# Local attention: the additive mask moved behind the score products, and cut to the key columns that it can change

## The chip, the cores and the metric

One core of a Trainium2 chip runs the whole program. The metric is the device time of one launch, in microseconds (us), lower is better. The kernel is a chain of eight stages, a small transformer with a residual stream of 2048 tokens x 256 features that stays in the on-chip memory. The change touches one of them, the fifth in order of execution, causal local attention.

## The reference

The stage takes the normalised residual `x` as query and `ctx_1024` as key and value (8 batches, 256 tokens, 16 heads of width 16, window 64). A block of 64 queries sees its own block of 64 keys and the one before it; key j is hidden from query i if j comes later than i, and for the first block of a batch the whole previous block is hidden.

```python
qb = q.reshape(b, h, nb, w, d) * scale            # w = 64, nb = 4
kw = look_around(kb)                              # [.., 128, d]: the block before, then the own block
vw = look_around(vb)
mask = (t[:, :, None] >= kt[:, None, :]) & (kt[:, None, :] >= 0)
sim = jnp.einsum('bhnwd,bhnjd->bhnwj', qb, kw)
sim = jnp.where(mask[None, None], sim, -jnp.finfo(sim.dtype).max)
attn = jax.nn.softmax(sim, axis=-1)
out = jnp.einsum('bhnwj,bhnjd->bhnwd', attn, vw)
...
return x @ W_out.T + b_out
```

So of the 128 key columns of a block, the first 64 are hidden altogether or not at all, and only the last 64 have the diagonal mask.

## The kernel before

The stage is `stage_local_attention` (L1930 to L2290). A step n covers two neighbouring query blocks of one batch: batch b = n // 2, u = n % 2, 16 steps in all. In a step the heads lie in four row groups r of 32 partitions (`RT = 4`), so the score products use 32 rows of the array; each row group has a PSUM bank of its own, `scores[r]`, of 128 x 512: partitions are two heads x 64 queries, columns are four (block, half of the features) pairs j x 128 keys. The four banks are handled in two halves, r = 0, 1 (half 0) and r = 2, 3 (half 1), so there are 32 score halves in all.

All steps are written out, without a loop on the chip. `walk` fixes the order on every engine. In one turn of it for step n:

```python
score(n, 1); turn(n, 0)
score(n + 1, 0)
if u == 0: prep_x(b + 1)
weigh(n - 1)
if u == 0: prep_k(b + 1)
turn(n, 1)
if u == 1 and b >= 1: final(b - 1)
if u == 0 and b >= 2: finish(b - 2)
```

- `score` (L2057): TensorE. It waits for the spread queries (`q_ready`), and for each bank until ScalarE has read it. Per bank it first writes the mask with one matmul of a bf16 identity against `masks[:, u > 0]` (L2066, 128 rows, 512 columns, start=True), and then adds eight fp32 score records onto it (L2072: four matmuls, each two passes in the trace; 32 rows, 128 columns; the two banks of a half take turns).
- VectorE takes the negated maximum of each of the four column groups of a bank (L2184), ScalarE the exponentials (L2142, four of 128x128 to a bank).
- `turn` (L2082): eight fp32 128x128 transposes in a half, into one of two `turned` banks each; ScalarE copies them out (L2151, to `eT`).
- `weigh` (L2099): 128 small fp32 records, 128 rows x 32 columns of the array, values and row sums, into the bank `av`; then VectorE takes reciprocals (L2191) and the quotient (L2193).
- `prep_x`, `prep_k` (L2053): four 128x128 transposes of the next batch's queries or keys into the one `misc` bank; `final` (L2112) the output product of the batch before; `finish` on VectorE normalises two tiles (L217) and takes their largest values (L2212).

On VectorE the order is that of `walk` too; on ScalarE it is exponents(n, 1), the copies of turn(n, 0), the queries of prep_x, exponents(n + 1, 0), the keys of prep_k, the copies of turn(n, 1).

Of the kernel before, what the change touches and what calls it, by code (L numbers as in the profile page):

```python
# [12 lines left out]
P = 128  # L13
# [14 lines left out]
KD = D // P  # L28
# [1901 lines left out]
def stage_local_attention(nc, core, ins):  # L1930
# [4 lines left out]
    HEADS, W = 16, 64  # L1935
# [9 lines left out]
    with ExitStack() as ctx:  # L1945
# [4 lines left out]
        ident16 = st.sb("ident16", [P, P], BF16)  # L1950
        masks = st.sb("masks", [P, 2, 4, P], BF16)
# [4 lines left out]
        qd = st.sb("qd", [P, 2, KD, NU, 2 * W])  # L1956
        kT = st.sb("kT", [P, 2, KD, W + S])
# [17 lines left out]
        def walk(prep_x, prep_k, score, turn, weigh, final, finish):  # L1975
            prep_x(0)
            prep_k(0)
            score(0, 0)
            for n in range(STEPS + 1):
                b, u = divmod(n, NU)  # L1980
                if n < STEPS:
                    score(n, 1)
                    turn(n, 0)
                if n + 1 < STEPS:
                    score(n + 1, 0)
                if u == 0 and b + 1 < B:
                    prep_x(b + 1)
                if n >= 1:
                    weigh(n - 1)
                if u == 0 and b + 1 < B:  # L1990
                    prep_k(b + 1)
                if n < STEPS:
                    turn(n, 1)
                if u == 1 and b >= 1:
                    final(b - 1)
                if u == 0 and b >= 2:
                    finish(b - 2)
            final(B - 1)
            finish(B - 1)
# [4 lines left out]
        @block.sync  # L2004
        def _(sp):
            wm = Walk(misc, sp)
            ctx_d = ins["ctx_1024"]

            def load(b):
                sp.dma_start(xs[:, b % 2, 0:2, :], core.xn[:, 2 * b:2 * b + 2, :]).then_inc(xs_in[b % 2], 16)  # L2010
                sp.dma_start(xs[:, b % 2, 2:4, :], ctx_d.rearrange("b (h p) d -> p b h d", p=P)[:, b, :, :]
                             ).then_inc(xs_in[b % 2], 16)
                if b >= 2:
                    sp.wait_ge(vz_ready, b - 1)
                sp.dma_start(vn[W:P, b % 2, 0, :], ctx_d[b, 0:W, :]).then_inc(vn_in[b % 2], 16)
                for nb in range(1, UNITS):
                    sp.dma_start(vn[:, b % 2, nb, :], ctx_d[b, W * (nb - 1):W * (nb + 1), :]).then_inc(vn_in[b % 2], 16)

            sp.wait_ge(const, 3)
            load(0)  # L2020
            sp.dma_start(wo[:, :, :], ins["L2_xattn_W_out"].rearrange("(r p) k -> p r k", p=P)).then_inc(small_in, 16)
            sp.dma_start(bias[:, :], ins["L2_xattn_b_out"].partition_broadcast(P)).then_inc(small_in, 16)
            load(1)
            wm.skip(1)

            def prep_k(b):
                wm.when_filled(wm.use())
                if b + 2 < B:
                    load(b + 2)

            walk(lambda b: wm.skip(1), prep_k, nothing, nothing, nothing, lambda b: wm.skip(1), nothing)

        @block.tensor
        def _(pe):
            ws, wt, wa, wm = (Walk(banks, pe) for banks in (scores, turned, av, misc))
            pe.wait_ge(const2, 2)
            kept, score_bank, turned_bank = {}, {}, {}

            def weights():
                pe.wait_ge(small_in, 32)  # L2040
                ps, filled, _ = wm.fill()
                for kt in range(KD):
                    for r in range(2):
                        last = nc.tensor.transpose(ps[:, (kt * 2 + r) * P:(kt * 2 + r + 1) * P],
                                                   wo[:, r, kt * P:(kt + 1) * P], core.ident[:, :])
                last.then_inc(filled, 1)

            def prep(b, part):
                pe.wait_ge(xs_in[b % 2], 32 * (b // 2 + 1))
                ps, filled, kept[b] = wm.fill()  # L2050
                for kt in range(KD):
                    for h in range(2):
                        last = nc.tensor.transpose(ps[:, kt * S + h * P:kt * S + (h + 1) * P],  # L2053
                                                   xs[:, b % 2, 2 * part + h, kt * P:(kt + 1) * P],
                                                   core.ident[:, :])
                last.then_inc(filled, 1)

            def score(n, half):
                b, u = divmod(n, NU)
                pe.wait_ge(q_ready, n + 1)  # L2060
                if u == 0 and half == 0:
                    wm.when_read(kept[b])
                banks = [(r, ws.fill()) for r in SETS[half]]
                for r, (ps, _, use) in banks:
                    score_bank[n, r] = use
                    nc.tensor.matmul(ps[:, :], ident16[:, :], masks[:, int(u > 0), :, :], start=True, stop=False)  # L2066
                for j in range(4):
                    nb, kt = divmod(j, KD)
                    lo = W * (NU * u + nb)
                    for r, (ps, filled, _) in banks:  # L2070
                        rows = slice(R * r, R * (r + 1))
                        last = nc.tensor.matmul(ps[:, j * P:(j + 1) * P], qd[rows, n % 2, kt, nb, :],  # L2072
                                                kT[rows, b % 2, kt, lo:lo + P], start=False, stop=(j == 3))
                        if j == 3:
                            last.then_inc(filled, 1)

            def turn(n, half):
                for r in SETS[half]:
                    ws.when_read(score_bank[n, r])
                    ps, filled, turned_bank[n, r] = wt.fill()  # L2080
                    for j in range(4):
                        last = nc.tensor.transpose(ps[:, j * P:(j + 1) * P], e[:, n % 2, r, j, :], core.ident[:, :])  # L2082
                    last.then_inc(filled, 1)

            def weigh(n):
                b, u = divmod(n, NU)
                pe.wait_ge(vz_ready, b + 1)
                for r in range(RT):
                    wt.when_read(turned_bank[n, r])
                ps, filled, _ = wa.fill()  # L2090
                for j in range(4):
                    nb, kt = divmod(j, KD)
                    for what in range(2):
                        o = (4 * what + j) * W
                        for h in range(2):
                            for r in range(RT):
                                lhs = (ones[:, h, :, :] if what else
                                       vz[:, b % 2, NU * u + nb, RT * kt + r, 2 * h:2 * h + 2, :])
                                last = nc.tensor.matmul(ps[R * r:R * (r + 1), o:o + W],  # L2099
                                                        lhs.rearrange("p a d -> p (a d)"),  # L2100
                                                        eT[:, n % 2, r, j, h * W:(h + 1) * W],
                                                        start=(h == 0), stop=(h == 1))
                last.then_inc(filled, 1)

            def final(b):

                if b == B - 1:
                    wa.when_all_read()
                ps, filled, _ = wm.fill()
                for h in range(2):  # L2110
                    for kt in range(KD):
                        last = nc.tensor.matmul(ps[:, h * D:(h + 1) * D], aoT[:, b % 2, kt, h * P:(h + 1) * P],  # L2112
                                                woT[:, kt, :], start=(kt == 0), stop=(kt == KD - 1))
                last.then_inc(filled, 1)

            weights()
            walk(lambda b: prep(b, 0), lambda b: prep(b, 1), score, turn, weigh, final, nothing)

        @block.scalar
# [1339 lines left out]
```

## Time and profile before

| | |
|---|---|
| median of 3 runs | 2153.23 us (2150.3 to 2153.67) |
| the profiled execution's own time | 2154.32 us |
| its span in the profile | 2152.6 us |
| mean granted TensorE clock | 0.937 of full speed |
| TensorE matmul busy, of the span | 87% |
| VectorE busy | 59% |
| ScalarE busy | 39% |
| GpSimd busy | 13% |

The span is that of the instructions in the trace, and the device time lies a little above it. In the profile PE is TensorE's matmuls, PEld its weight loads, DVE is VectorE, ACT is ScalarE, POOL is GpSimd. A matmul's duration in the trace reaches to the modelled arrival of its last result, so matmuls that follow each other overlap in the rows: with x records in a merged row, the last one starts at the row's start plus the row's length less one record's duration. The attention stage runs from about 1331 to 1477 us of the span.

### The profile page before, as it was taken

To read this page: it belongs to the slowest core of one execution; us is meant where nothing else is said; L and a number is where in the kernel's file an instruction comes from. 1 tells how busy PE (TensorE), PEld (TensorE's weight loads), DVE (VectorE), ACT (ScalarE), POOL (GpSimd) and SP (SyncE) were. 2 spreads that over 40 slices of the span, in tenths; PEclk is the share of its full clock that TensorE was granted. 3 is DMA by queue.
4 is the path that set the end of the run, shared out by engine and by line. 5 is a ranking of instruction groups with operands and counts; after the bars stand their busy time and mean duration, and the time that the engine had idled before them with its cause. 6 is when DMAs were issued, how large, how long until landed. Compare 5 with 4: busy or idle time off the path is not lost. (4 is left out here: it accounts for less than half of the span.)

```text
span 2152.6 us, 39260 instructions
## 1 busy us (share of the span) xinstructions
PE 1881.7 (87%) x13712; PEld 1521.6 (71%) x13713; DVE 1274.2 (59%) x4672; ACT 839.8 (39%) x2287; POOL 276.1 (13%) x501
## 2 busy tenths in 40 slices
PE   8699997999998989999999995996940977999978
PEld 6466665677667979999999884884520866777745
DVE  7767764877883541111111152775778527999988
ACT  3333334655653111111111112872477513444469
POOL 2001112000000160000000253330000230000022
PEclk9899998999998999999999996998975987999989
DMA  5111112121113431230320112201000031111100
GB/s 177 64 44 55 55 54 72 40 79 40 40 40 122 171 113 44 79 140 26 140 83 24 46 48 68 71 22 60 0 1 0 0 119 43 34 35 37 34 8 33
DMA packets 104818, 127.05 MB, mean 59 GB/s; under 512 B 32080, under 2 KB 83800, under 8 KB 102872
## 3 DMA queue, kind: packets, MB, share of 16 engines
q1 hardware_dynamic: 93512, 109.35, 15.3%
q0 software_dynamic: 3072, 8.39, 1.2%
q10 hardware_dynamic: 8080, 7.35, 1.0%
q8 instruction: 85, 1.39, 0.3%
q14 instruction: 69, 0.57, 0.1%
HBM read 86.39 MB, written 34.54 MB: 56 GB/s over the span
## 5 line engine op out<-in xcount | busy, mean ns | idle before, releaser
L1721 DVE TENSOR_TENSOR me_h<-me_sg,me_ps_u 128x512 f32<-128x512 f32 x106 | 72.6, 687 | 288.1 <-PE me_ps_u L1544 272.8
L1677 ACT ACTIVATE me_sg<-me_ps_g 128x512 f32<-128x512 f32 x106 | 63.3, 597 | 370.9 <-PE me_ps_g L1544 340.8
L1260 ACT ACTIVATE ca_e<-ca_scored,ca_neg_max 128x256 f32<-128x256 f32 x256 | 127.2, 499 | 108.3 <-DVE ca_neg_max L1319 108.3
L1544 PE MATMUL me_ps_g<-me_x_turned,me_w 128*128 128x128 f32 x1184 | 145.1, 276 | 1.9 <-issue 1.9
L1544 PE MATMUL me_ps_u<-me_x_turned,me_w 128*128 128x128 f32 x1184 | 145.4, 276 | 0.0
L1544 PEld LDWEIGHTS me_ps_g<-me_x_turned,me_w 128*128 128x128 f32 x1184 | 141.1, 192 | 4.6 <-issue 2.9
L1551 PE MATMUL me_ps_y<-me_w,me_h 128*128 128x256 f32 x592 | 140.0, 379 | 0.0
L1544 PEld LDWEIGHTS me_ps_u<-me_x_turned,me_w 128*128 128x128 f32 x1184 | 139.4, 193 | 0.0
L2922 ACT ACTIVATE sc_y_all<-ss_v 128x16 f32<-128x16 f32 x256 | 60.9, 238 | 159.9 <-DVE ss_v L2985 159.9
L1551 PEld LDWEIGHTS me_ps_y<-me_w,me_h 128*128 128x128 f32 x592 | 106.8, 190 | 11.4
L1319 DVE CUSTOM_DVE_ANT_0 ca_scored<-ca_main,ca_mask_add 128x256 f32<-128x256 f32 x256 | 92.9, 419 | 22.4 <-PE ca_main L1200 22.4
L3070 PE MATMUL ss_idle<-ident 128*128 128x128 f32 x648 | 90.5, 286 | 0.0
L2954 DVE SCALAR_TENSOR_TENSOR ss_left<-ss_nq,ss_v 128x16 f32<-128x16 f32 x446 | 90.3, 202 | 0.0
L2390 PE MATMUL ig_ps<-nw_int_wT,ig_xT 128*128 128x384 f32 x256 | 87.3, 496 | 0.0
L1922 POOL DMA_INDIRECT me_rows<-moe_y_list,me_slot x32 | 31.2, 974 | 432.9 <-DVE carrier L81 424.6
L3070 PEld LDWEIGHTS ss_idle<-ident 128*128 128x128 f32 x648 | 79.8, 196 | 6.5 <-issue 3.4
L2142 ACT ACTIVATE la_e<-la_scores,la_mx 128x128 f32<-128x128 f32 x256 | 70.5, 422 | 30.1 <-DVE la_mx L2184 30.1
L1212 PE MATMUL ca_turned<-ident,ca_e 128*128 128x128 f32 x512 | 70.2, 281 | 13.4 <-DVE ca_e L1332 13.4
L1745 DVE COPY me_y<-me_ps_y 128x256 f32<-128x256 f32 x37 | 15.7, 425 | 108.0 <-PE me_ps_y L1551 108.0
L1212 PEld LDWEIGHTS ca_turned<-ident,ca_e 128*128 128x128 f32 x512 | 57.8, 143 | 29.9 <-DVE ca_e L1332 22.2
L1332 DVE TENSOR_SCALAR ca_e<-ca_e,ca_rsums 128x256 f32<-128x256 f32 x256 | 74.9, 356 | 2.2
L1544 PE MATMUL me_ps_g<-me_xT,me_w13s 128*128 128x128 f32 x512 | 67.2, 284 | 5.6 <-issue 4.8
(441 smaller groups left out, 4392.9 us busy)
## 6 DMA issues: line engine op xcount, KB each, us to landing
me_w<-in_L_ffn_w_e SPq DMA_DIRECT2D x24, 1024.0 KB, 7.4
ss_gb<-scan_g_band SPq DMA_DIRECT2D x15, 512.0 KB, 3.7
ca_k_list<-kv_out SPq DMA_DIRECT2D x28, 256.0 KB, 2.4
ca_v_list<-kv_out SPq DMA_DIRECT2D x28, 256.0 KB, 2.4
moe_x_list<-me_zeros SPq DMA_DIRECT2D x1, 5248.0 KB, 21.8
me_x_tile<-moe_x_list SPq DMA_DIRECT2D x38, 128.0 KB, 2.0
moe_y_list<-me_y ACTq DMA_DIRECT2D x37, 128.0 KB, 1.7
ca_kT<-ca_k_list SPq DMA_DIRECT2D x4, 1024.0 KB, 5.2
```

Source lines behind the costliest of these rows:

```text
L1212: last = nc.tensor.transpose(ps[:, jt * S + it * P:jt * S + (it + 1) * P], e[:, g % 3, e_, it, jt * P:(jt + 1) * P], core.ident[:, :])
L1260: nc.scalar.activation(e[:, g % 3, e_, it, :], scored[:, g % 2, e_, it, :], ACT.Exp, scale=-1.0, bias=neg_max[:, g % 2, n:n + 1], accum_ou ...
L1319: last = nc.vector.tensor_tensor_reduce(scored[:, g % 2, e_, it, :], ps[:, it * S:(it + 1) * S], mask_add[:, b, :], -1.0, -NEG, ALU.add, A ...
L1332: last = nc.vector.tensor_scalar(e[:, g % 3, e_, it, :], e[:, g % 3, e_, it, :], rsums[:, par, n:n + 1], None, ALU.mult)
L1544: last = nc.tensor.matmul(ps[:, j * P:(j + 1) * P], w[:, n, kt, f:f + P], x[:, kt, :], start=(kt == 0), stop=(kt == KD - 1))
L1551: last = nc.tensor.matmul(ps_y[:, 0:D], h[:, c, j, :], w[:, f, :], start=(f == 0), stop=(f == FT - 1))
L1677: nc.scalar.activation(sg[:, c, :], ps_g[c][:, :], ACT.Silu).then_inc(done, 1)
L1721: nc.vector.tensor_tensor(h[:, c, :, :].rearrange("p j n -> p (j n)"), sg[:, c, :], ps_u[c][:, :], ALU.mult).then_inc(done[c], 1)
L2142: last = nc.scalar.activation(e[:, n % 2, r, j, :], scores.ps[r][:, j * P:(j + 1) * P], ACT.Exp, bias=mx[:, n % 2, r, j:j + 1])
L2390: last = nc.tensor.matmul(ps[2 * w + c][:, 0:HALF], xT[:, par, kt, :], wT[:, w, kt, c * HALF:(c + 1) * HALF], start=(kt == 0), stop=(kt == ...
L2954: return nc.vector.scalar_tensor_tensor(out, nq[:, t % 2, :].unsqueeze(2).broadcast_to([P, C, n]), 1.0, src, ALU.add, ALU.mult)
L3070: nc.tensor.matmul(idle[:, 0:P], core.ident[:, :], core.ident[:, :], start=True, stop=True)
```

## The change

The mask matmul of each bank moves from ahead of the score matmuls to behind them, and writes only columns that can be masked. In the last 64 keys of each of the four column groups the diagonal mask is added, a matmul with 4 x 64 = 256 columns, in every bank. In steps with u = 0 a second matmul of 2 x 64 = 128 columns hides the block before the first one. The first score matmul now starts the accumulation, and the last mask matmul ends it and signals `filled`.

```diff
                 for r, (ps, _, use) in banks:
                     score_bank[n, r] = use
-                    nc.tensor.matmul(ps[:, :], ident16[:, :], masks[:, int(u > 0), :, :], start=True, stop=False)
                 for j in range(4):
                     nb, kt = divmod(j, KD)
                     lo = W * (NU * u + nb)
                     for r, (ps, filled, _) in banks:
                         rows = slice(R * r, R * (r + 1))
-                        last = nc.tensor.matmul(ps[:, j * P:(j + 1) * P], qd[rows, n % 2, kt, nb, :],
-                                                kT[rows, b % 2, kt, lo:lo + P], start=False, stop=(j == 3))
-                        if j == 3:
-                            last.then_inc(filled, 1)
+
+                        nc.tensor.matmul(ps[:, j * P:(j + 1) * P], qd[rows, n % 2, kt, nb, :],
+                                         kT[rows, b % 2, kt, lo:lo + P], start=(j == 0), stop=False)
+
+                for r, (ps, filled, _) in banks:
+                    columns = ps[:, :].rearrange("p (j s) -> p j s", j=4)
+                    last = nc.tensor.matmul(columns[:, :, W:2 * W], ident16[:, :], masks[:, 1, :, W:2 * W],
+                                            start=False, stop=(u > 0))
+                    if u == 0:
+                        last = nc.tensor.matmul(columns[:, 0:KD, 0:W], ident16[:, :], masks[:, 0, 0:KD, 0:W],
+                                                start=False, stop=True)
+                    last.then_inc(filled, 1)
```

## Rows read from the trace of the kernel before

**Rows 1.** The head of the profile's page

```profile
span 2152.6 us, 39260 instructions
```

**Rows 2.** Busy time by stretches of the stage: us, then busy us of each engine

```profile
1331.00:1345.00 14.00, 12.93 (x88) 9.19 (x90) 3.87 (x6) 8.59 (x30) 5.50 (x9) 0.67 0.28 86
1345.00:1360.00 15.00, 14.99 (x370) 12.31 (x368) 9.42 (x12) 13.66 (x45) 5.01 (x8) 1.00 0.20 66
1360.00:1375.00 15.00, 15.00 (x366) 12.57 (x363) 9.58 (x19) 11.19 (x37) 4.08 (x10) 1.00 0.20 59
1382.00:1399.00 17.00, 16.85 (x380) 13.91 (x376) 13.12 (x23) 13.31 (x44) 6.23 (x11) 1.00 0.19 61
```

**Rows 3.** Groups of instructions of the stage: score and mask matmuls

```profile
L2072 PE MATMUL la_scores<-la_kT,la_qd 32*128 32x128 f32 x512 | 39.1, 293 | 0.0
L2066 PE MATMUL la_scores<-la_masks,la_ident 128*128 128x512 bf16 x64 | 20.4, 402 | 0.8 <-ACT la_kT L2135 0.8
```

**Rows 4.** Timeline of TensorE around one score half: start us, length us, engine

```profile
1386.49 1.09 PE L2082 MATMUL la_turned<-ident,la_e 128*128 128x128 f32 x8
1387.42 0.59 PE L2066 MATMUL la_scores<-la_masks,la_ident 128*128 128x512 bf16 x2
1387.95 1.16 PE L2072 MATMUL la_scores<-la_kT,la_qd 32*128 32x128 f32 x16
1389.04 0.66 PE L2053 MATMUL la_misc<-ident,la_xs 128*128 128x128 f32 x4
...
1387.31 0.21 PEld L2066 LDWEIGHTS la_scores<-la_masks,la_ident 128*128 128x128 bf16 x2
1387.94 0.97 PEld L2072 LDWEIGHTS la_scores<-la_kT,la_qd 32*128 32x128 f32 x16 [0.42 <-issue]
...
1389.62 0.27 PEld L2099 LDWEIGHTS la_av<-la_eT,la_vz 128*32 128x32 f32 x16 [0.17 <-issue]
```

**Rows 5.** Timeline of TensorE in two other stages: short bf16 matmuls

```profile
728.57 0.22 PE L1641 MATMUL me_ps_r<-me_both,me_before 128*128 128x128 bf16 x1
728.62 0.22 PE L1642 MATMUL me_ps_r<-me_both,me_ones 128*128 128x128 bf16 x1
...
728.57 0.10 PEld L1642 LDWEIGHTS me_ps_r<-me_both,me_ones 128*128 128x128 bf16 x1
...
2101.61 1.03 PE L3223 MATMUL bt_ps_yo<-nw_bit_wdT,bt_hT 128*128 128x256 bf16 x8
```

**Rows 6.** Timeline of one batch: from one weigh to the turn after the next

```profile
1391.21 0.41 PE L2099 MATMUL la_av<-la_eT,la_ones 128*32 128x64 f32 x16
1391.55 0.42 PEld L2053 LDWEIGHTS la_misc<-ident,la_xs 128*128 128x128 f32 x4
1391.68 1.76 DVE L2191 RECIPROCAL la_rsum<-la_av 128x256 f32<-128x256 f32 x1 [1.26 <-PE la_av L2099]
...
1395.71 1.27 DVE L2184 TENSOR_REDUCE la_mx<-la_scores 128x4 f32<-128x512 f32 x2
...
1396.42 2.17 ACT L2142 ACTIVATE la_e<-la_scores,la_mx 128x128 f32<-128x128 f32 x8 [1.59 <-DVE la_mx L2184]
1398.43 1.13 ACT L2151 ACTIVATE la_eT<-la_turned 128x512 f32<-128x512 f32 x2
...
1398.66 0.41 PE L2099 MATMUL la_av<-la_eT,la_ones 128*32 128x64 f32 x16
...
1399.19 0.91 PEld L2082 LDWEIGHTS la_turned<-ident,la_e 128*128 128x128 f32 x8 [0.28 <-issue]
```

**Rows 7.** Timeline: the weight loads of the same turn one batch earlier

```profile
1382.16 0.91 PEld L2082 LDWEIGHTS la_turned<-ident,la_e 128*128 128x128 f32 x8 [0.28 <-issue]
```

**Rows 8.** Timeline of TensorE in the first steps of the stage

```profile
1334.24 1.03 PE L2066 MATMUL la_scores<-la_masks,la_ident 128*128 128x512 bf16 x2
1335.20 2.08 PE L2072 MATMUL la_scores<-la_kT,la_qd 32*128 32x128 f32 x16
1337.21 1.97 PE L2082 MATMUL la_turned<-ident,la_e 128*128 128x128 f32 x8
```

## Prediction

> **What bounds the kernel now.** The head of the page gives the span, 2152.6 us [rows 1]; the execution's own time is 2154.32 us, 1.7 us more, and the median 2153.23 us. The reader should see first how small the stage's share is: it runs for about 145 us, and the mask matmuls are 64 records of 0.40 us on average, 20.4 us of overlapping busy time [rows 3]. Then the stretches: once the clock has risen, TensorE's matmuls cover 14.99 of 15.00 and 15.00 of 15.00 us, and 16.85 of 17.00 us later; VectorE is busy 13.12 and ScalarE 13.31 of those 17.00 us [rows 2]. TensorE looks like the limit, but the missing 0.15 us in each batch from 1382 us on is where to look.
>
> Third, the timeline of one batch. A load that has to wait for the array alone starts about 0.07 us before the row in front of it ends: weigh ends at 1391.21 + 0.41 = 1391.62, and the next load is at 1391.55 [rows 6]. The later weigh ends at 1398.66 + 0.41 = 1399.07, and the load of turn(n, 1) comes at 1399.19, 0.19 us later than it could. What ended last there is the ScalarE copy from 1398.43, which frees a `turned` bank. Back from it: copies after exponents (1396.42, after 1.59 us of idling for the maxima), maxima at 1395.71, behind the quotient and `finish`, behind the reciprocal at 1391.68, behind the end of the weigh before [rows 6]. So one loop closes each batch: from the end of weigh(n - 1) to turn(n + 1, 1) it goes over VectorE and ScalarE and takes 1399.19 - 1391.62 = 7.57 us whatever TensorE does; from there to the next weigh(n - 1) it is pure TensorE. The batch's distance is 1399.19 - 1382.16 = 17.03 us [rows 6, 7], so the TensorE part is 9.46 us.
>
> I name the score halves of this cycle in TensorE's order: A = score(n, 1) with u = 0; B = score(n + 1, 0), u = 1; C = score(n + 1, 1), u = 1; D = score(n + 2, 0), u = 0. A and B lie in the TensorE part, before weigh; C and D lie beside the VectorE and ScalarE part.
>
> **The change part by part.** One half before: masks from 1387.42, scores' first load at 1387.94, next load at 1389.04 [rows 4].
>
> *Mask in front removed.* The transposes end at 1386.49 + 1.09 = 1387.58, so the first score load, which changes the tile from 128 to 32 rows, can start at 1387.51 by the same 0.07 us. Such a step from 128x128 to a smaller tile is seen once, from prep_x to weigh: 1389.04 + 0.66 - 0.07 = 1389.63 against 1389.62 [rows 4]. Against 1387.94 that is -0.43 us in every half.
>
> *Mask behind added.* A 512-column mask costs 0.59 - 0.38 = 0.21 us of stream [rows 4]; half the columns, 0.11 us as an estimate. Eight matmuls of 256 columns in another stage take 1.03 us together, results included, which fits [rows 5]. For 128 columns two neighbours start 0.05 to 0.06 us apart, 728.57 and 728.62 [rows 5]. After a mask an fp32 transpose comes no sooner than its load, (1.09 - 0.66) / 4 = 0.11 us [rows 4]. The change of tile behind the scores is there before and after, and the exposed first load too. So B and C add 0.11 + 0.11 = 0.22 us: -0.21 us net. A has four masks: 0.11 + 0.06 + 0.11 + 0.11 = 0.39 us, net -0.04, say -0.05 us. D is followed by weigh, so it gets one more change of tile: 0.06 for the first load, 0.28 to the last mask, 0.22 - 0.07 = 0.15 to the load of weigh, 0.49 in all: +0.05 us. A batch's TensorE work falls by 0.42 us.
>
> *Where it lies on the path.* From 1382 us on, only A and B count: -0.26 us a batch. C's 0.21 less D's 0.05 become a longer wait at turn(n + 1, 1), 0.19 + 0.16 = 0.35 us. The loop has five such TensorE parts left (1382, 1399, 1416, 1433 and 1450 us): -1.3 us. From 1346 to 1374 us nothing waits [rows 2], and D, A, B, C, D, A, B count in full: 0.10 - 0.10 - 0.63 = -0.63 us. The first halves run at a granted clock of 1.2 GHz (0.67 of full speed on average over 1331 to 1345 us [rows 2], the lower level first): 1334.24 to 1337.21 is 2.97 us for a half of kind A, 0.96 of it in front of the scores [rows 8]. Behind them the masks cost at the doubled rate 0.21 + 0.11 + 0.21, plus loads: an estimate of -0.15 us for each of two A halves and -0.2 us for the first B. C after it stands before a ScalarE copy and gives nothing. Together -0.5 us. Sum: -1.3 - 0.63 - 0.5 = -2.4 us.
>
> *What is free.* 32 more mask matmuls bring 32 more loads of the identity; they hide behind the mask matmul before. If they did not, each would cost its 0.10 us, 3.2 us if all were on the path, and about 1.1 us for the eleven A and D halves on it, times two banks: 2.2 us. The Trainium skill, "TensorE: Matmul & The Clock Gate", section on packing small matmuls, says that a weight load overlaps with matmuls under way only where its row group differs, which speaks against the change. The rows say otherwise: the load of L1642 starts at 728.57 with the matmul before it, also 128 rows, and the two matmuls are 0.05 us apart although the load lasts 0.10 us [rows 5]. By the rule the total would be -2.4 + 2.2 = -0.2 us, by the rows it is -2.4 us. The first bank of a half is ready a little earlier than before, the second up to 0.1 us later in A, but VectorE's first maximum (0.64 us a bank) covers that. No DMA, no other queue moves.
>
> *Not shown before:* a mask that reads and writes runs of 64 with gaps. Below: the columns' own rate. Above: twice the time, 0.21 and 0.11 us. Then B costs 0.1 and A 0.2 us more, A + B is +0.05 us a batch, and the whole about +1 to +2 us. I take the column rate, because that is the one that the nearest rows, masks and matmuls without gaps, show.
>
> **The rivals.**
> 1. *All of TensorE's gain arrives* because the 7.57 us loop has room that I don't see. Then -0.42 x 7 - 0.5 = -3.5 us; with the clock rising one score half sooner, about 1 us more, -4.5 us. For it: TensorE is busy 99%. Against it: the 0.19 us wait stands in every batch.
> 2. *Nothing arrives:* exposed loads or gapped runs at half rate, -0.2 to +2 us. Against it for the loads: [rows 5]. Open for the runs.
> 3. *The granted clock falls inside the stage* (slower). The wide bf16 masks go down from 512 to 256 columns, and the wait grows; before the stage warmed up, TensorE ran for 6 us at 1.2 GHz although it was busy all the time with just these masks and scores [rows 8]. A half takes 2.97 us there against 1389.04 - 1387.31 = 1.73 us at 2.4 GHz [rows 4], +1.2 us. It decides from six halves of 32 on: 7.2 - 2.4 = +4.8 us. Against it: the clock was 1.00 in all stretches, also with the waits [rows 2].
> 4. *The change does nothing to see* is within rival 2.
>
> **How the numbers follow.** From 2153.23: 2153.23 - 2.4 = 2150.8 us. A measurement of this kernel can tell about 0.2%, 4.3 us. Forecast (-1 to -4 us): 0.66. Rival 2: 0.14. Rival 1, with the part past -4.3 us from the clock: 0.14. Rival 3: 0.06. Range: the low end takes rival 1 (2149) and the scatter of the three runs, about 1.5 us; the high end takes the gapped runs at half rate, +2 us: 2147.8 to 2155.2 us. The forecast and rival 2 are both within 0.2%. Faster by over 0.2%: 0.14, within 0.2%: 0.80, slower by over 0.2%: 0.06.
>
> **What the profile of the changed kernel would show.** Mask groups: 64 matmuls of 256 and 32 of 128 columns, 0.27 and 0.22 us long; 0.38 would mean half rate. Starts of masks 0.11 and 0.06 us apart: loads hidden. First score load about 0.20 us behind the last transpose's start. Distance of turn(n + 1, 1) from batch to batch 16.77 us, its load about 0.28 us past the end of weigh instead of 0.12. ScalarE's idle time before the exponents of C falls from 1.59 to about 1.3 us. Granted clock 1.00 from 1346 to 1466 us. Wrong if the distance is 16.6 us or less (rival 1) or 17.0 or more (rival 2), or if the stage shows a clock under 1.

## The result, and the profile after

In 14 runs of each on one chip, the changed kernel took 2162.9 us (median; 2154.57 to 2166.66) and the kernel before 2152.97 us: ratio 1.0047, 95% interval 1.0033 to 1.0062. I had forecast 2150.8 us and no measurable change; it is slower by more than 0.2%, above the range. A second measurement on another chip, 8 runs beside 24 of the kernel before, gave 1.0031 (1.0018 to 1.0043). The profiled execution took 2163.56 us.

The head of the page, against [rows 1], and its row of the queue that brings TensorE's instructions (packets, MB, share of 16 engines):

```profile
span 2161.8 us, 39324 instructions
...
q8 instruction: 85, 1.39, 0.3%
```

64 instructions more: 32 matmuls and their weight loads. 1.39 MB in 85 packets is about 16 KB, one block of instructions, in each fetch. The row is the same in the kernel before: no more is fetched, and what can differ is where in the work a fetch falls. From its first score load to the end of its last `final`, the stage takes 152.2 us instead of 145.9. What stands in front of it takes 0.95 us less in this profile, what stands behind it 3.9 us more.

First what I forecast locally. TensorE around one score half with u = 1, against [rows 4]:

```profile
1388.93 0.71 PE L2089 MATMUL la_turned<-ident,la_e 128*128 128x128 f32 x5
1389.57 1.16 PE L2072 MATMUL la_scores<-la_kT,la_qd 32*128 32x128 f32 x16
1390.66 0.39 PE L2077 MATMUL la_scores<-la_masks,la_ident 128*128 128x256 bf16 x2
1390.89 0.60 PE L2053 MATMUL la_misc<-ident,la_xs 128*128 128x128 f32 x4
...
1390.66 0.11 PEld L2077 LDWEIGHTS la_scores<-la_masks,la_ident 128*128 128x128 bf16 x2
```

The two cut masks take 0.39 us from the first start to the last end, one takes 0.27, so the second starts 0.12 us behind the first: their columns' own rate, the gaps of 64 cost nothing, and the load of the identity is hidden. All that holds. Now a weigh of an even step (u = 0): it follows half D and is the second weigh in the cycle of [rows 6]. TensorE again, later in the stage:

```profile
1434.05 0.28 PE L2077 MATMUL la_scores<-la_masks,la_ident 128*128 128x256 bf16 x1
1434.17 0.22 PE L2080 MATMUL la_scores<-la_masks,la_ident 128*128 128x128 bf16 x1
1434.23 0.27 PE L2077 MATMUL la_scores<-la_masks,la_ident 128*128 128x256 bf16 x1
1434.34 0.22 PE L2080 MATMUL la_scores<-la_masks,la_ident 128*128 128x128 bf16 x1
1434.48 0.43 PE L2106 MATMUL la_av<-la_eT,la_vz 128*32 128x64 f32 x16
...
1435.85 0.39 PE L2106 MATMUL la_av<-la_eT,la_vz 128*32 128x64 f32 x13
1436.96 0.25 PE L2106 MATMUL la_av<-la_eT,la_vz 128*32 128x64 f32 x2 [0.71 <-issue]
```

Thirteen matmuls into a row of sixteen, TensorE stops for 0.71 us, and the releaser is "issue": nothing that the profile shows was waited for. In the kernel before all 16 weighs have 1.78 us between their first and last start. Here those of steps 6, 8, 10, 12 and 14 have 2.54, 2.64, 2.78, 2.51 and 4.00 us. What moved in that time is in the view of the DMA queues over 1433 to 1438 us, 0.125 us a column (then queue, packets, MB):

```profile
DMA  0000000000500000000000000000000000000000
GB/s 0 0 0 0 0 0 0 0 0 0 131 0 0 0 0 0 0 0 0 0 0 0 0 0 0 0 0 0 0 0 0 0 0 0 0 0 0 0 0 0
...
q8 instruction: 1, 0.02, 1.4%
```

One fetch of instructions begins at about 1434.3 us, just as weigh begins, and TensorE goes on 2.7 us later. An undisturbed weigh issues all of its 256 loads and matmuls in 1.78 us, less time than that. Five such places lie 767 to 769 TensorE records apart, three blocks of 256. A batch was 773 records (matmuls, weight loads and 21 waits for semaphores) and is now 781: the difference is the change's.

The batches themselves, by the weight loads of the turn behind that weigh, one batch apart:

```profile
1401.96 0.86 PEld L2089 LDWEIGHTS la_turned<-ident,la_e 128*128 128x128 f32 x8
...
1419.62 0.86 PEld L2089 LDWEIGHTS la_turned<-ident,la_e 128*128 128x128 f32 x8
```

17.66 us, where it was 17.03 [rows 6, 7] and I had forecast 16.77. By the first load of `final`, the seven distances of the stage were 17.02, 17.03, 17.03, 17.03, 17.35, 15.85 and 6.26 us; they are 17.28, 17.55, 17.66, 17.79, 17.67, 16.52 and 8.11: 5.0 us more in all.

Last the start of the stage, windows as in [rows 2], cut where the clock rises (in the kernel before at 1340.3 us):

```profile
1330.31:1349.60 19.29, 18.48 (x116) 15.63 (x118) 5.15 (x8) 11.40 (x38) 7.58 (x12) 0.50 0.35 103
1349.60:1360.00 10.40, 10.40 (x332) 9.15 (x331) 6.11 (x9) 8.60 (x28) 0.42 (x1) 1.00 0.02 5
```

The granted clock was 0.50 (1.2 GHz) for 19.3 us of the stage instead of 9.0, and the first weigh started 20.4 us behind the stage's start instead of 17.0. Is this a cost of the change, or chance?

### The profile page after: what moved, and what is told of

The parts are those of the page before. It is cut to its first block and busy times, and to the rows that moved or that the text cites. A ratio compares the mean times of both kernels' runs of the same rounds, so it can differ in the third digit from the quotient of the medians.

```text
span 2161.8 us, 39324 instructions
## 1 busy us (share of the span) xinstructions
PE 1888.1 (87%) x13744; PEld 1532.6 (71%) x13745; DVE 1276.2 (59%) x4672; ACT 840.8 (39%) x2287; POOL 276.2 (13%) x501
## 3 DMA queue, kind: packets, MB, share of 16 engines
q8 instruction: 85, 1.39, 0.3%
```

## The experiments

Three questions: do the stalls come from where blocks of instructions end, and is that all; why does less TensorE work not shorten a batch; is the late clock the change's. "Empty instruction" below is a TensorE nop. The kernel before was measured beside each group, and each group ran on another chip: its medians are 2139.64, 2150.53 and 2139.41 us, so only ratios are compared between groups. First, the changed kernel with the fetches moved:

```diff
+            for _ in range(192):
+                nc.tensor.nop("pad", nofuse=True)
             pe.wait_ge(const2, 2)
             kept, score_bank, turned_bank = {}, {}, {}
```

> The changed kernel with 192 TensorE no-operations ahead of the stage's first instruction, where TensorE waits for the masks anyway. Nothing of the stage's work changes; only the place of the 256-instruction blocks in its code does (the trace of the changed kernel shows instruction fetches of 16384 bytes, and five stalls inside weigh whose places are 767 to 769 TensorE records apart). Theory 1, code fetch: the added 32 mask matmuls moved a block boundary into weigh, whose 256 records run in 1.78 us while a fetch takes over 2 us; with the boundary elsewhere the stalls inside weigh (0.7 to 0.9 us in each batch from 1400 us on) are gone, the distance from batch to batch falls from 17.5 to 17.8 us to 16.8 to 17.2 us, and the total by 3 to 4 us. Theory 2, the new order of masks and scores itself causes the wait (banks, semaphores): distance stays at 17.5 us or more. Of the granted clock at the start of the stage neither says anything: if it rises at 1349 us again, that part of the loss (about 3 us) stays.

2136.23 us against 2139.64, ratio 0.9986 (0.9972 to 1.0). Only the weigh of step 1 stalls (2.83 us), none from step 2 on; distances 17.03, 17.02, 17.03, 17.02, 17.13, 15.61, 6.26 us; stage 145.0 us. 192 instructions more, and the loss is gone: by the ratios 0.45% against the second measurement of the change, more than the 3 to 4 us that I expected.

The same instructions at the end of the stage instead, so that all later stages stand in the code as above, but this one as in the changed kernel:

```diff
             walk(lambda b: prep(b, 0), lambda b: prep(b, 1), score, turn, weigh, final, nothing)
+            for _ in range(192):
+                nc.tensor.nop("pad", nofuse=True)
```

> The changed kernel with 192 TensorE no-operations behind the stage's last instruction, so that the code of the later stages lies at the same place within its 256-instruction blocks as before the change (64 + 192 = 256), and the stage itself is left as it is. If the later stages lost their 3.8 us (from the end of the attention stage to the end of the span: 679.7 us against 675.8) because their code moved, they get it back and the total falls by about 3 to 4 us; if that part is chance or the granted clock, the total stays within 1.5 us of the changed kernel. In the stage nothing changes: distance 17.5 to 17.8 us, stalls in weigh.

2147.41 us, ratio 1.0037 (1.0024 to 1.0049). The weighs stall, distances 17.35 to 18.22 us; the stage takes 149.0 us, and what stands behind it 681.1 us, the most in any profile. So the loss comes with this stage's place in the code; putting the later stages' code back to its place within the blocks (64 + 192 = 256) doesn't heal it.

Masks behind the scores, but whole, with no instruction added:

```diff
+                for r, (ps, filled, _) in banks:
+                    nc.tensor.matmul(ps[:, :], ident16[:, :], masks[:, int(u > 0), :, :], start=False, stop=True
+                                     ).then_inc(filled, 1)
```

> The mask behind the scores, but whole: one matmul of 512 columns for each bank, as many instructions as before the change. Code-fetch theory: no stall inside weigh, distance 17.0 to 17.2 us (TensorE's share of the batch is as before: 0.43 us less in front, 0.42 us more behind), total within 1.5 us of before. Order theory: stalls in weigh as in the changed kernel, 17.5 us or more. Clock: if the order of masks and scores is what delays the rise of the granted clock (1349.6 us against 1340.3), it is delayed here too, and the stage's first 20 us are about 3 us longer; if the cut to fewer columns is what delays it, the rise comes as before.

Ratio 0.999 (0.9976 to 1.0005), no stall, distances 17.04 to 17.06 for the first four. The order alone does nothing. Then the kernel before with none of the change, its code moved by 48 instructions at the start of the stage:

```diff
+            for _ in range(48):
+                nc.tensor.nop("pad", nofuse=True)
             pe.wait_ge(const2, 2)
```

> The kernel before the change, with 48 TensorE no-operations ahead of the stage's first instruction. Its block boundary lies just behind weigh (a stall of 0.3 us in the turn behind it at 1451 us); 48 instructions earlier it lies inside weigh. Code-fetch theory: stalls of 0.7 to 1 us inside the second weigh of each batch although the masks are untouched, distance 17.5 us instead of 17.03, total +2 to +4 us. Rival: the stalls come only with the new order, so nothing changes here, distance 17.03, total within 1 us.

2146.02 us, ratio 1.003 (1.0016 to 1.0044), each second weigh from step 2 to 12 takes 2.76 to 3.36 us, distances 17.84 to 18.37 for the first five: a loss as large as that of the change in its second measurement, without the change.

Now the second question. With the fetches moved, a batch still takes 17.02 us. TensorE over one batch, the kernel before and the padded one:

```profile
1382.16:1399.19 17.03, 16.88 (x376) 13.91 (x376) 13.12 (x24) 13.34 (x43) 6.23 (x11) 1.00 0.19 61
```

```profile
1375.11:1392.13 17.02, 16.50 (x380) 14.02 (x380) 13.50 (x24) 13.33 (x43) 6.22 (x12) 1.00 0.20 60
```

Its busy time fell by 0.38 us, the distance by 0.01. VectorE has 0.38 us more. VectorE and GpSimd in the kernel before, and in the padded one, from the reciprocal on:

```profile
1391.68 1.76 DVE L2191 RECIPROCAL la_rsum<-la_av 128x256 f32<-128x256 f32 x1 [1.26 <-PE la_av L2099]
1393.48 0.42 DVE L2193 TENSOR_TENSOR la_aoT<-la_av,la_rsum 128x256 f32<-128x256 f32 x1
1393.82 1.32 DVE L217 TENSOR_SCALAR x_norm<-x_res,la_ln_mean_var,la_ln_rstd 128x256 f32<-128x256 f32 x2
1395.05 0.73 DVE L2212 TENSOR_REDUCE nw_x_max<-x_norm 128x1 f32<-128x256 f32 x2
...
1393.51 1.47 POOL L2278 TENSOR_TENSOR x_res<-x_res,la_bias 128x256 f32<-128x256 f32 x2
```

```profile
1371.95 1.76 DVE L2200 RECIPROCAL la_rsum<-la_av 128x256 f32<-128x256 f32 x1 [1.21 <-PE la_av L2108]
1373.74 0.42 DVE L2202 TENSOR_TENSOR la_aoT<-la_av,la_rsum 128x256 f32<-128x256 f32 x1
1374.08 1.70 DVE L217 TENSOR_SCALAR x_norm<-x_res,la_ln_mean_var,la_ln_rstd 128x256 f32<-128x256 f32 x2
1374.16 1.47 POOL L2287 TENSOR_TENSOR x_res<-x_res,la_bias 128x256 f32<-128x256 f32 x2
1375.71 0.73 DVE L2221 TENSOR_REDUCE nw_x_max<-x_norm 128x1 f32<-128x256 f32 x2
```

In the kernel before GpSimd's bias additions start 0.31 us ahead of the pair of x_norm, in the padded kernel 0.08 us behind it. The pair takes 1.70 us instead of 1.32, and the first of it ends 0.15 us behind GpSimd's first addition in both kernels. So VectorE's chain, which now starts earlier, is held back to GpSimd's, and GpSimd's own time, as I read the waits, comes round another way: la_xT copied by ScalarE, `spread`, the copy of vz, the bias, and then the maxima and exponents of half C, from which the next round starts. To test it, the bias additions go ahead of that wait:

```diff
+            def add_bias(b):
+                for h in range(2):
+                    nc.gpsimd.tensor_tensor(core.x[:, 2 * b + h, :], core.x[:, 2 * b + h, :], bias[:, :], ALU.add
+                                            ).then_inc(bias_added, 1)
             def prep_x(b):
+                if b >= 1:
+                    add_bias(b)
                 wm.when_read(wm.use())
                 spread(NU * b)
```

(They leave their old place; batch 0 keeps its own.) With it in the padded changed kernel:

> The changed kernel with the 192 no-operations in front, and GpSimd's bias additions to the residual (two per batch) moved ahead of its wait for the queries, into its idle time, for all batches but the first. Padding alone gave a distance of 17.02 us: the reciprocal started 0.26 us earlier, but the first normalisation on VectorE took 0.96 instead of 0.58 us and ended 0.15 us behind GpSimd's first bias addition, as before. Theory (port loop): the batch is bound by a loop over final, maxima of A, exponents, queries' copy, GpSimd's spread, value copy and bias addition, and the normalisation that waits for it; without the additions there the normalisations take about 0.5 us each, and the distance falls to 16.4 to 16.6 us, TensorE's own work: total 3 to 4 us under the padded kernel, about -0.3% against before. Rival: the distance has another bound (ScalarE, semaphores): it stays at 16.9 us or more, total as with padding alone.

Ratio 1.0001 (0.9983 to 1.0019), but the distances are 16.77, 16.77, 16.77, 16.77, 16.84, 15.61 and 6.26 us, each x_norm 0.40 us long. So the additions were in a loop of the batch, but I had expected 16.4 to 16.6 us and 0.3% off the total, and neither came. The clock rose 23.8 us after the stage's start in this profile. The same move in the kernel before:

> The kernel before the change with only the bias additions moved as above. Port loop theory: TensorE's stream has just 0.19 us of waiting in each batch, so the distance falls from 17.03 only to 16.84 us, and the total by about 1.2 us (-0.05%, not to be told from 0). If it falls further, TensorE's stream wasn't full; if it stays, the additions weren't in a loop.

Ratio 1.0003 (0.9989 to 1.0017), distances 16.78, 16.78, 16.78, 17.32, 17.31: here, too, the additions were 0.25 us of each batch (I had expected 0.19), and from the fourth on a stop in the turn behind weigh, 0.55 us from one load's start to the next and again "issue", gives it back.

The change without its added instructions, one mask matmul per bank:

```diff
+                for r, (ps, filled, _) in banks:
+                    columns = ps[:, :].rearrange("p (j s) -> p j s", j=4)
+                    if u == 0:
+                        last = nc.tensor.matmul(ps[:, :], ident16[:, :], masks[:, 0, :, :], start=False, stop=True)
+                    else:
+                        last = nc.tensor.matmul(columns[:, :, W:2 * W], ident16[:, :], masks[:, 1, :, W:2 * W],
+                                                start=False, stop=True)
+                    last.then_inc(filled, 1)
```

> The changed order, masks behind the scores, but one mask matmul for each bank: 256 columns where u = 1, and the whole mask (512 columns) where u = 0. So it has the 64 mask matmuls of the kernel before and its place of fetch blocks. Code-fetch theory: no stall in weigh, distance 17.0 to 17.1 us, total within 0.15% of before. If cutting the mask or its gapped runs cost something by themselves, it shows as 17.3 us or more.

Ratio 0.9992 (0.9975 to 1.0009), no stall, distances 17.02 to 17.04 for the first four. With the early additions on top:

> One mask matmul for each bank behind the scores (as in the run with one mask) and the bias additions moved. TensorE's work in a batch: B and C 0.21 us less each than before, A about 0, D about 0.15 more, so 0.27 us less than the 16.84 us of a full stream: distance 16.55 to 16.65 us, no stall in weigh, total about -0.15 to -0.2% against before. With a stall in weigh the distance is over 17 us.

Ratio 0.9986 (0.9972 to 1.0), distances 16.87 to 16.88. I had expected 16.55 to 16.65. In its trace TensorE waits about 0.2 us ahead of prep_k and 0.3 us behind half C in every batch; the section on the prediction comes back to these two waits.

The last group settles cause and chance. The kernel before, made as long as the changed one in the same score halves (the empty instructions stand ahead of the scores there, the added masks behind them), and nothing else:

```diff
                     nc.tensor.matmul(ps[:, :], ident16[:, :], masks[:, int(u > 0), :, :], start=True, stop=False)
+                    for _ in range(2 if u == 0 else 0):
+                        nc.tensor.nop("pad", nofuse=True)
```

> The kernel before with two empty TensorE instructions behind the mask matmul of each u = 0 bank: 64 in all, the same instruction count per batch as the changed kernel and nothing else of the change. Theory (the distance in instructions between fetches falls on weigh): TensorE stalls of 0.5 to 1.3 us inside each second weigh, distances of the `final` loads of 17.4 to 17.8 us instead of 17.03, and 3 to 5 us more in the stage, so about +0.2%. Rival (the stalls come from the masks behind the scores themselves): distance stays 17.03 to 17.1, ratio 1.000.

2146.28 us against 2139.41, ratio 1.0032 (1.0018 to 1.0046). TensorE in weigh:

```profile
1421.40 0.39 PE L2101 MATMUL la_av<-la_eT,la_vz 128*32 128x64 f32 x13
1422.58 0.25 PE L2101 MATMUL la_av<-la_eT,la_vz 128*32 128x64 f32 x2 [0.78 <-issue]
```

The same stop behind a thirteenth matmul. The weighs of steps 6, 8, 10, 12 and 14 stop behind exactly the same records, counted over TensorE's whole program, as in the changed kernel; the last weigh stops too. Distances 17.67, 17.62, 17.78, 17.85, 17.87. And the changed kernel once more:

> The changed kernel once more, for its ratio on this chip beside the others and for a second profile of the start of the stage. Theory: ratio 1.003 to 1.006, distances again 17.3 to 17.8 us with stalls in the second weigh of each batch. When the clock rises at the start is open: again about 19 us after the stage starts if the order of masks and scores sets it, or 7 to 9 us, as in the kernel before, if it is chance from execution to execution. Rival: ratio within 0.1% of 1 and no stalls (the first measurement was a matter of that chip).

2143.93 us, ratio 1.0031. The first five distances repeat to 0.01 us (17.28, 17.55, 17.65, 17.79, 17.66), the last two are 0.28 us shorter each (16.24, 7.84). But the clock rose 6.9 us after the stage's start, and the stage took 148.6 us instead of 152.2:

```profile
1310.77:1317.70 6.93, 6.90 (x48) 5.98 (x48) 2.58 (x4) 3.04 (x12) 2.85 (x5) 0.50 0.48 144
1317.70:1330.00 12.30, 11.38 (x232) 9.46 (x232) 5.57 (x7) 12.12 (x40) 4.69 (x7) 1.00 0.26 82
```

Now the changed kernel with three things at once: 200 empty instructions at the start of the stage, the early additions, and the masks of steps 0 and 1 whole and in front, as before the change. Of the last, the line that does it:

```diff
                     score_bank[n, r] = use
+                    if n < 2:
+                        nc.tensor.matmul(ps[:, :], ident16[:, :], masks[:, int(u > 0), :, :], start=True, stop=False)
```

> The changed kernel with three things: the masks of steps n = 0 and 1 in front and whole, as before (the cold start as before), the cut masks behind in all others; GpSimd's bias additions of batches 1 to 7 ahead of its wait in prep_x; and 200 empty TensorE instructions at the start of the stage, which put the fetches where the padded run had them. Theory: distances of 16.77 us as in the padded run with early additions, clock rising 7 to 9 us after the stage starts instead of 24, the stage at 142 to 144 us, so a ratio of 0.997 to 0.999. Rival (the rise of the clock has nothing to do with the order of masks and scores): rise again 17 us or later, stage 148 us, ratio 1.000.

Ratio 1.0011 (1.0 to 1.0022), distances 16.78 to 16.79 as expected, and the rival right about the clock: it rose 24.7 us after the start. And the padded kernel with early additions again, unchanged:

> The padded changed kernel with early bias additions once more: same file as before. It tells whether the late rise of the clock (24 us after the stage starts) belongs to the kernel or to one execution. Theory (belongs to one execution): the rise comes at another time in this profile, and where it comes at 7 to 9 us the stage is 143 to 144 us. Rival (belongs to the kernel): 24 us again, stage 148 us. Ratio 0.997 to 1.001 either way; distances 16.77 us in both.

2136.68 us against 2139.41, ratio 0.9986 (0.9974 to 0.9998). The clock rose after 8.0 us, the stage took 141.3 us instead of 148.1, and the distances are the same to 0.01 us. Windows of its start and of one batch:

```profile
1318.76:1326.80 8.04, 8.01 (x54) 6.77 (x56) 2.58 (x4) 4.15 (x16) 4.21 (x7) 0.50 0.38 122
1326.80:1340.00 13.20, 12.30 (x242) 10.36 (x238) 6.95 (x10) 11.65 (x36) 4.71 (x7) 1.00 0.25 78
1368.28:1385.05 16.77, 16.42 (x387) 14.03 (x381) 12.53 (x23) 13.33 (x44) 6.17 (x11) 1.00 0.20 62
```

This version of the change has the shortest batches. It is 0.1% under the kernel before here and level with it in its first measurement: nothing to tell from no change.

## Why the prediction was wrong

**Which step failed: "What is free".** I asked of the 32 added matmuls only whether their weight loads hide. They do. But they are 64 more instructions, eight a batch, and TensorE's instructions come in blocks. In the kernel before no stop falls inside a weigh, so the ends of blocks lay where a fetch had time. In the changed one, one lies inside each second weigh of the steady part, and the five stalled weighs are longer than 1.78 us by 0.76, 0.87, 1.00, 0.73 and 2.23 us, 5.6 us in all, on the path: the term that I put at nothing is larger than my whole forecast of -2.4 us. That this, and not the masks, makes the loss is shown from three sides: the change with the fetches moved (0.9986), the kernel before with only its code moved (1.003), and the kernel before with only the length added (1.0032). The five measurements with stalled weighs throughout the steady part have ratios of 1.003 to 1.0047; the eight without lie at 0.9986 to 1.0011.

The Trainium skill, "Runtime: NRT & Kernel Launch", section "Instruction fetch mechanics", says that instructions come in blocks of 256 and that the cost of crossing from one to the next is "mostly hidden". The first part agrees with the 16 KB fetches and the stops 767 to 769 records apart. The second holds for most of this stage, and not in weigh, where 256 records last 1.78 us. All 30 stops inside weighs, in the five profiles that have them throughout, ended 2.2 to 2.9 us after the start of a fetch. I had not weighed this rule, since I had not asked what instruction count does.

**"The change part by part": the work was about right.** I forecast 0.42 us less TensorE work in a batch; busy time fell from 16.88 to 16.50 us with the fetches moved, and to 16.42 us with the early additions too. Mask durations of 0.27 and 0.22 us, starts 0.12 us apart, and the first score load at 0.20 us behind the last transpose's start were as forecast. Rival 2, exposed loads or half rate, fell, though its sign came: the distance is over 17.0 us, for another reason. ScalarE's idle time before the exponents of C didn't fall to 1.3 us; it is 1.58 us at 1433.84 us.

**"Where it lies on the path": one loop too few.** I said that VectorE and ScalarE take 7.57 us "whatever TensorE does", and gave the change 0.26 us of the 9.46 us in which TensorE works alone. With the fetches moved, the second part is 9.05 us, even more than forecast, but the first is 7.97 us, and the batch gains 0.01 us. Within the first lie two x_norm that GpSimd's bias additions slow down, and GpSimd's start hangs on another loop, which was tied with the first at 17.02 us.

With the additions moved away the distance is 16.77 us, my number, but not by my argument: the move alone gives the kernel before 16.78, so of this pair, too, the change makes 0.01 us. The parts are 7.38 and 9.40 us in the kernel before, 7.76 and 9.01 us in the changed one. What TensorE saves it spends in two waits that only the changed kernel has. Both end with a ScalarE copy: one ahead of prep_k, which needs the one `misc` bank back, and one ahead of the turn behind half C, as I read it for a `turned` bank:

```profile
1377.52 0.63 PE L2055 MATMUL la_misc<-ident,la_xs 128*128 128x128 f32 x4 [0.23 <-ACT la_xT L2139]
...
1379.66 1.24 ACT L2160 ACTIVATE la_eT<-la_turned 128x512 f32<-128x512 f32 x2
1380.05 0.39 PE L2079 MATMUL la_scores<-la_masks,la_ident 128*128 128x256 bf16 x2
1380.56 1.11 PE L2091 MATMUL la_turned<-ident,la_e 128*128 128x128 f32 x8
```

In the first timeline above prep_x starts 0.11 us behind the last mask; this turn starts 0.39 us behind it, its weight loads 0.11 us after the first of the two copies ends. Both waits stand in the padded kernel without the move as well. So the batch has a third chain, over VectorE's maxima of half A and ScalarE's work up to that copy; it was read off the trace, and no run takes it away. That 16.77 came out exactly is luck. In [rows 6] I followed one chain back to where it closed, and took the durations on it as given. I didn't ask which of them another engine sets, nor what else ends within 0.1 us of it.

**Rival 3: the clock.** Between its rise and the end of the stage it fell once, at 1472.4 us for 3.4 us, and it does the same in the kernel before (1473.4 us), so the rival, as I put it, didn't happen. But when it rises at the start varies from 6.9 to 24.7 us over all the profiles, and by 12 and 16 us between two profiles of the same kernel (19.3 and 6.9; 23.8 and 8.0). In those two pairs the later rise goes with 3.6 and 6.8 us more in the stage. That is scatter of the execution, as large as everything that the change could give. Every run has at least its mean granted clock over the whole program on record, and within one kernel a thousandth less of it goes with 1.4 to 1.7 us more time (a straight line through the runs of each group). In the second measurement the changed kernel had 0.9371 on average and the kernel before 0.9385, which goes with about 2 of the 5.4 us between their means; by that line 3.6 us remain at equal clock, 6.1 to 9.7 us in the three other versions with stalled weighs, and -3.7 to +0.6 us in the eight without (estimates, each with a standard error of about 0.8 us). In the first measurement the changed kernel had 0.9335; the clocks of the 14 runs beside it are not on record, so the clock's part in 1.0047 against 1.0031 stays open. I priced the start at -0.5 us, which no profile here can confirm or refute.

**How large the loss is.** Over all profiles, the stage takes 152.1 us on average in the five with stalled weighs (148.6 to 156.1) and 145.2 us in the nine without, the kernel before among them (141.3 to 149.9): 7.0 us, where the ratios of the changed kernel say 6.7 to 10 us. But the clock rose late, 17 to 25 us into the stage, in three of the five and in two of the nine. Among profiles with an early rise, the two with stalls take 148.8 us on average, and the four without stalls and without moved additions 144.8: 4 us, near the 5.0 us by which the distances differ.

**What stays open.** Behind the stage the same five profiles have 677.7 us on average (674.2 to 681.1), the nine 675.0 (672.1 to 676.2). The two sets overlap, and the run with the padding at the end, whose later code lies within its blocks as in the kernel before, has the longest time there (681.1 us); no run separates them further, so whether some 2.7 us of the loss lie there is not settled; the clock, which has long stretches at 1.2 GHz there in every kernel, is a possible carrier. When the clock rises at the stage's start is not explained either, only that the place of the masks doesn't decide it: it was late, 17.2 us, also in both versions of the kernel before with empty instructions.

## What to carry to other kernels

In a long unrolled program, adding instructions is not free even where each hides behind work: before counting a gain of under 1%, look for stretches where an engine issues 256 instructions faster than a fetch comes back, and for stops with the releaser "issue" in a row of equal instructions. If a change shifts these, measure it with a few empty instructions ahead as well, or the measurement is of the place and not of the change. And where one loop closes each batch with 0.1 to 0.2 us of slack elsewhere, look for the second loop before counting a gain on the first: an instruction on the path whose duration differs from run to run of the same work (x_norm at 0.58 and 0.96 us, 0.40 alone) may be one that another engine times.

## What the runs showed of the hardware

A fetch of one 16 KB block of instructions took 0.9 to 1.5 us by its packet, and 2.2 to 2.9 us until the stalled engine went on; 256 short TensorE instructions are issued in 1.78 us. Weight loads of 128 rows hide behind matmuls of the same 128 rows: cut masks with their loads start 0.12 and 0.055 us apart. VectorE's x_norm (128 x 256, fp32) takes 0.40 us alone and up to 0.98 us beside a GpSimd addition of the same size. The granted clock at the start of one and the same kernel's stage can rise 7 or 19 us into it, with the work in front unchanged.
